# Two graph-attention layers on one core: VectorE compares the places with a column held in PSUM instead of one in SBUF

## The reference

```python
# layer 0                                     # layer 1
q, k, v = proj(layernorm(x))                  q, k, v, skip = proj(x)
e = sum(q[dst] * k[src]) / 4                  e = sum(q[dst] * (k[src] + edge @ We)) / 4
p = exp(e - segment_max(e, dst)[dst])         the same
alpha = p / segment_sum(p, dst)[dst]          the same
agg = segment_sum(alpha * v[src], dst)        agg = segment_sum(alpha * (v[src] + edge @ We), dst)
x = x + agg @ Wo, then a gelu FFN             layernorm(agg + skip + x), gelu FFN, layernorm
```

## Time and profile before

| | us |
|---|---|
| median of 3 runs (lowest, highest) | 1789.74 (1785.43, 1793.72) |
| profiled execution: its span, first to last instruction | 1423.2 |
| between that span and the median | 366.5 |
| busy in the span: PE, DVE | 1072.8, 1076.5 |
| busy in the span: ACT, POOL | 840.3, 901.0 |
| edge stage of layer 0, first gather to last | 65.9 to 596.6 |
| edge stage of layer 1, first gather to last | 752.1 to 1284.6 |

### The profile page before, as it was taken

One profiled execution on the slowest core, in us unless ns is written; L12 is line 12 of the kernel. 1 busy time (PEld: TensorE's weight loads), 2 busy tenths in 40 slices (PEclk: granted clock), 3 DMA queues, 4 the chain that ended last, 5 costly groups with the idle time before them and its releaser, 6 DMA issues. The chain is left out here.

```text
span 1423.2 us, 28503 instructions
## 1 busy us (share of the span) xinstructions
PE 1072.8 (75%) x6809; PEld 956.7 (67%) x6809; DVE 1076.5 (76%) x2695; ACT 840.3 (59%) x2605; POOL 901.0 (63%) x1028
## 2 busy tenths in 40 slices
PE   3937678767877787768896788888888888887790
PEld 1436677667866776758735677787787778776690
DVE  5538877787877787865443888988988898897557
ACT  1615776676667666644443467766776676576351
POOL 2177777777777777531046777777777777770453
PEclk9967877787777777778897989999999999898795
DMA  5385555555555565420024567667766766671001
GB/s 157 106 182 178 173 188 194 191 155 189 193 186 159 192 193 171 137 91 0 7 79 141 176 211 223 197 193 220 214 199 196 224 207 189 219 229 48 1 1 45
DMA packets 100659, 222.50 MB, mean 156 GB/s; under 512 B 34875, under 2 KB 49882, under 8 KB 96941
## 3 DMA queue, kind: packets, MB, share of 16 engines
q0 software_dynamic: 39936, 109.11, 26.8%
q1 hardware_dynamic: 57927, 109.78, 22.8%
q10 hardware_dynamic: 2662, 2.05, 0.5%
HBM read 184.86 MB, written 36.00 MB: 155 GB/s over the span
## 5 line engine op out<-in xcount | busy, mean ns | idle before, releaser
L464 POOL DMA_INDIRECT KV<-kv_table,idx x832 | 810.3, 974 | 301.5 <-issue 247.4
L732 PE MATMUL PS<-QT,OHT 128*128 x1664 | 401.6, 330 | 146.5 <-DVE OHT L990 122.3
L732 PEld LDWEIGHTS PS<-QT,OHT 128*128 128x128 f32 x1664 | 317.9, 236 | 166.1 <-issue 164.6
L733 PE MATMUL PS<-QT,OHT 128*128 x1664 | 390.4, 324 | 0.0
L733 PEld LDWEIGHTS PS<-QT,OHT 128*128 128x128 f32 x1664 | 319.1, 238 | 0.0
L592 ACT ACTIVATE AGG<-AGG,PC,RCS x800 | 309.3, 387 | 3.1 <-ACT AGG L588 2.4
L1008 DVE TENSOR_TENSOR PR<-KV,PS 128x512 f32<-128x512 f32 x208 | 140.6, 676 | 105.6 <-DMA KV<-kv_table,idx 103.7
L778 PE MATMUL PS<-OH,KV 128*128 128x128 f32 x1600 | 208.4, 280 | 2.9 <-DVE OH L1110 1.2
L588 ACT ACTIVATE AGG<-PS 128x127 f32 x800 | 208.0, 260 | 1.0 <-issue 0.7
L778 PEld LDWEIGHTS PS<-OH,KV 128*128 128x128 f32 x1600 | 196.7, 197 | 5.6 <-issue 2.6
L584 ACT ACTIVATE PC<-PS 128x4 f32<-128x4 f32 x200 | 33.5, 168 | 267.1 <-PE PS L778 256.0
(11 more groups left out here) (158 smaller groups left out, 1352.2 us busy)
## 6 DMA issues: line engine op xcount, KB each, us to landing
REL<-rel_dram SPq DMA_DIRECT2D x52, 512.0 KB, 4.4
window_dram<-OH SPq DMA_DIRECT2D x25, 1024.0 KB
OH<-window_dram SPq DMA_DIRECT2D x50, 512.0 KB, 6.1
KV<-kv_table,idx POOLq DMA_INDIRECT x832
EA<-in_edge_batch SPq DMA_DIRECT2D x52, 256.0 KB
kv_table<-KV SPq DMA_DIRECT2D x52, 128.0 KB, 1.7
X<-in_x SPq DMA_DIRECT2D x2, 832.0 KB, 10.1
GATES<-edge_gates SPq DMA_DIRECT2D x8, 208.0 KB, 10.0
```

The costliest lines, as they stand in the source:

```text
L464: g.indirect_dma_start(KV[:, s, j, :], None, kv_table, bass.IndirectOffsetOnAxis(ap=idx[:, s, j:j + 1], axis=0)).then_inc(gathered[s][hh], 16)
L732: te.matmul(o, OHT[:, q // 2, 0, e0:e0 + P], QT[:, ds(blk, P)], start=True, stop=False)
L733: last = te.matmul(o, OHT[:, q // 2, 1, e0:e0 + P], QT[:, ds(blk + P, P)], start=False, stop=True)
```

## The change

VectorE copies `iota_part` once to PSUM (two columns of bank 7 that nothing else uses), and `one_hots1` compares `REL` with a column of that copy, spread over the 1024 entries. The instruction is a `tensor_tensor` of two inputs where it was a `tensor_scalar` of one input with a number per partition. Its result is the same, it stands at the same place in the order, and it releases the same semaphore. There are 52 such instructions a layer. One wait for the copy is added ahead of the first of them.

```diff
+        part_psum = PS[7][:, 384:386]
...
             v.tensor_reduce(dsel[:, :], ident[:, :].rearrange("p (h j) -> p j h", h=H), AX.X, ALU.add).then_inc(S["prep_step"], 1)
+            v.tensor_copy(part_psum, iota_part[:, :]).then_inc(S["part_kept"], 1)
             split_biases(0, 3)
...
                     for nf in range(2):
-                        yield v.tensor_scalar(OHT[:, 0, nf, :], REL[:, 0:8 * P], iota_part[:, nf:nf + 1], None,
+                        yield v.tensor_tensor(OHT[:, 0, nf, :], REL[:, 0:8 * P], part_psum[:, nf:nf + 1].broadcast_to([P, 8 * P]),
                                               ALU.is_equal).then_inc(S["oht_ready"], 1)
...
                 dve.wait_ge(S["rel_stored"], 32)
+                dve.wait_ge(*done("part_kept", 1))
                 for ins in one_hots1(0):
                     pass
```

More of the change, by code:

```diff
@@ L175, in build @@
             rel_loaded gate_loaded windows_stored last_loaded out_stored""".split()}
-        counts = """we_zeroed consts_made rel_made gate_made prep_step kv_copied kv_free gates_made loops_step seen_step iota_kept
+        counts = """we_zeroed consts_made rel_made gate_made prep_step kv_copied kv_free gates_made loops_step seen_step iota_kept part_kept
             pool_go sp_go stat_step moment_step var_ready sd_ready rs_ready
```

## The result

| | us |
|---|---|
| before, measured beside the change: median of 4 (lowest, highest) | 1791.08 (1785.43, 1793.72) |
| after: median of 4 (lowest, highest) | 1809.93 (1799.63, 1815.79) |
| ratio, 95% interval | 1.0105 [1.006, 1.015] |
| after, the profiled execution: its time, its span | 1799.63, 1797.9 |

The change makes the kernel 19 us slower, 1.05%, and the interval leaves out 1. The forecast was 1798 with a range of 1783 to 1815, and slower as the likeliest side. Time and side lie inside of it, but the second half of the table says that one step under the forecast is wrong: only 1.7 us of this execution lie outside of its span, not some 366. The span before was 1423.2, and the span after is 1797.9.

The account below looks back on a forecast made before the run. It took POOL's gathers to bound layer 0 and a VectorE-TensorE ring layer 1. Terms of -10.0, +0.5, -0.6, +19.6, -1.3 and +0.15 made +8.3 us, so 1789.7 became 1798, range 1783 to 1815.

Parts of the forecast that it names:

- The 366.5 us outside of it stay: Whole kernel: measured time outside the profiled span was taken as unchanged, turning a span of 1431.5 into 1798 us.
- The sum of +8.3: Profiled execution: -10.0 + 0.5 - 0.6 + 19.6 - 1.3 + 0.15 us, giving a span of 1431.5.
- New form, 0.83 a round dearer: VectorE's two one-hots per round: start to start, the new instructions cost 0.35 and 0.48 us more.
- the ring: Layer 1: VectorE from L1001 through both one-hots to AL, then TensorE to the next L1001; 20.50 us a round.
- The 1.2 a round: VectorE's one-hots: alternative cost from the skill's cycle formula, 0.60 us more each; total 8 to 9 us higher.
- It frees the gathers: POOL: gathers beside a one-hot, held up 0.28 us each by the old form, would not be by the new.
- Rival 4: Both layers: the new form holds POOL up as before, layer 0 gains nothing; +18 us, 1808; chance 0.05.
- Layer 0 gains 10.0: Layer 0, where POOL sets the pace: 400 gathers falling to the 0.946 median would save 10.0 us.
- Layer 1 loses 19.6: Layer 1: one second one-hot (0.48) plus 23 rounds at 0.83 us more, 19.6 us lost.
- rival 3: Layer 1: POOL sets the pace there too, so it gains some 10 us; 1769, faster; chance 0.09.
- rival 1: Layer 1: TensorE, waiting longer for one-hots, loses its higher clock; 1.15 us a round, 1811 to 1825; chance 0.22.
- the term of the clock: Layer 1: TensorE's low-clock stretch, costing about 1.7 us a round, might move; left unfixed and outside the forecast total.

Follow-up runs that it names:

- the pair of layer 0 and SBUF column: Against the kernel before: the new one-hot in layer 0 alone, 1421.67 us; the new form in both layers with its column read from SBUF, 1460.25 us.
- the pair with the ten products: Ten unused 128x128 TensorE products before layer 1's wait for AL, added to the change (1817.21 us) and to the kernel before (1798.21 us), on one chip.

## Why the prediction was right, and where it was wrong

**"The 366.5 us outside of it stay": wrong, and the step that failed.** The trace was of the prompt way, the times were of the late one. On the prompt chip span and time differ by 1.8 us, in the result by 1.7. The sum of +8.3 was made on a timeline that the measured executions did not follow, and carried to their median as if something fixed lay between. The page of the profile named no work in which 366 us could lie, and that was the warning.

**New form, 0.83 a round dearer: right.** 1203 ns beside L1112's 1217, a short round of 21.43 against 21.33 (most of the others: 21.25 to 21.46), and the part of the ring up to L754 grown from 15.2 to 16.0 to 16.2. The 120 + 1024 cycles of the Trainium skill (VectorE: DVE Perf Modes, the TRN2 errata) give 1192, and the 1203 agrees with it. It is not PSUM that this shows, since the column in SBUF gave 1211. The 1.2 a round that the prediction drew from the same section is above the 0.8 to 1.0 of the ring.

**It frees the gathers: right.** 947 ns in the mean of all. Rival 4 is out, by the result and by the pair of layer 0 and SBUF column.

**Layer 0 gains 10.0: right on the prompt chip in mechanism, a little large.** 7.5 us of the stage. The term brought every gather down to the median of 0.946, but with the new form in layer 0 their mean there is 0.953 (0.972 before). On late chips POOL stands for slots, and freeing it gained nothing: 654.9 us with the change and 654.1 with the old one-hots on one and the same chip.

**Layer 1 loses 19.6: right in mechanism, too small.** The ring is there, and rival 3 is out: POOL does run ahead. But rival 1, given 0.22, holds as well, in nine of 21 rounds: 31 us by the medians, of which 23 x 0.83 = 19 are the one-hots and nine times 1.15 = 10 the clock. What fell short is the term of the clock, which the sum put at nothing and the prediction named as what it couldn't fix. By parts the prompt chip would show some 28 to 30 us in all, 1.02; the whole change was not measured there.

**The number.** Measured 1809.93 for 1798. That it fell into the range was luck. On a late chip the sum's gain in layer 0 is absent, and its loss in layer 1 is there (18.7 us in the pair with the ten products), but not for the reason given, since there TensorE's releases come late and neither the ring of 20.5 nor POOL's 20.0 sets a round. By how much layer 1 loses without the ten products is not shown: it is 723.4 us in the trace after and 713.6 in the kernel before on another late chip, but 711.3 with the change on the chip of 1779.18. The whole change costs 0.4 to 1.05% there, and why the dearer one-hots cost time in a late round stays open. The signs of both ways agree; the argument did not describe the runs that were timed.

## What to carry to other kernels

Set the span of a trace beside the times measured (here they are 1.7 to 1.8 us apart in one and the same execution, in both ways), and if they differ by much more, treat the trace as another way of running: conclusions about who waits for whom don't carry over. In this kernel an instruction on VectorE that takes both inputs from SBUF, or the shorter one-input form, lengthened indirect gathers that ran beside it (1.87 and 1.23 us for 0.95); two inputs with one of them in PSUM avoid that, and pay in VectorE's own time (1203 ns for 766), so use it only in a stage that POOL bounds (here layer 0, 0.9972 where layer 1 gave 1.0237). Before tightening an engine's issue further, see whether others wait far beyond the work that releases them: here 288 us of waiting, put where it broke up the runs of gathers, made the kernel on a late chip 2% faster than before and 3% faster than the change alone.

## What the runs showed of the hardware

- One and the same kernel ran in 1425 us on one chip and in 1779 to 1793 on others, with the same instructions at the same durations (L990 766 and 746 ns, gathers 974 and 964); the difference lies in the edge stages alone (outside of them 145.2 and 124.8 us late, 148.2 and 125.2 prompt). There VectorE and ScalarE start late what needs TensorE's work (at 136.8 us for work that ended at 86.0), and the profile puts the idle time down to "remote" or "issue".
- A `tensor_tensor` with two SBUF inputs stretched a gather's issue from 0.95 to 1.87 us in the case shown, 1.01 in the mean of all; with a PSUM column it did not (0.94, 0.95); the old `tensor_scalar` stretched it to 1.23.
- With a ring of 20.5 us the low stretch of TensorE's clock was 3.4 us in nearly every round of layer 1; with 21.3 it was 3.4 and 6.8 by turns, and TensorE's part of the ring took 5.3 and 6.4 us.
